# Routing arithmetic placed in fewer attention steps, lane marks spread over more of them, and the first expert gathers issued one step later

## What is computed

```python
def attn(x):                       # one head, no mask
    q, k, v = x @ wq.T, x @ wk.T, x @ wv.T
    q, k = rope(q), rope(k)        # the first token is not rotated
    w = softmax(q @ k.T / sqrt(128))
    return (w @ v) @ wo.T

def ffn(z):
    for _ in range(2):
        zn = rmsnorm(z) * norm_w
        scores = softmax(zn @ router_w)
        top2 values, normalised to sum 1 -> cw (per token and expert)
        z = z + sum_e cw[:, e] * ((silu(zn @ w1[e]) * (zn @ w3[e])) @ w2[e])
    return z

x = x + layernorm(attn(layernorm(x)))
x = x + layernorm(ffn(layernorm(x)))
```

## Time and profile before

| | |
|---|---|
| Time, three runs | 1088.16, 1090.71, 1094.11 us; median 1090.71 |
| Profiled execution | 1088.16 us, span 1086.4 us |
| Busy share of the span | TensorE 91%, VectorE 64%, ScalarE 51%, GpSimd 47% |
| Mean granted TensorE clock | 0.971 |
| Stretch of the change | from about 268 to 378 us, in the span's own time |

### The profile page before, as it was taken

One profiled execution on the slowest core, in us unless ns is written; L12 is line 12 of the kernel. 1 busy time (PEld: TensorE's weight loads), 2 busy tenths in 40 slices (PEclk: granted clock), 3 DMA queues, 4 the chain that ended last, 5 costly groups with the idle time before them and its releaser, 6 DMA issues.

```text
span 1086.4 us, 22670 instructions
## 1 busy us (share of the span) xinstructions
PE 988.0 (91%) x7114; PEld 682.0 (63%) x7114; DVE 696.0 (64%) x1628; ACT 551.9 (51%) x1075; POOL 508.3 (47%) x671
## 2 busy tenths in 40 slices
PE   4899998869999899999999999999989999999930
PEld 2578877547787667666667765667656666666620
DVE  5879987958998555784435567545596333856336
ACT  3566666538888645433334564345644333333313
POOL 2412233775777763434443354443434444554315
PEclk9999999979999999999999999999999999999975
DMA  9900000000000144334336445356344335746342
GB/s 309 368 21 0 0 0 1 1 5 25 16 19 15 31 112 121 90 78 99 88 106 167 132 116 129 88 137 175 76 117 125 89 93 130 204 106 155 81 158 93
DMA packets 137350, 105.28 MB, mean 97 GB/s; under 512 B 84528, under 2 KB 124080, under 8 KB 137264
## 3 DMA queue, kind: packets, MB, share of 16 engines
q1 hardware_dynamic: 123632, 66.88, 23.6%
q0 software_dynamic: 13632, 37.24, 11.6%
HBM read 54.27 MB, written 31.20 MB: 79 GB/s over the span
## 4 chain that ended last, share of the span: by engine, by line
PE 78%; DVE 13%; issue 3%; POOL 2%; ACT 2%; DMA 1%; SPq 0%; DVEq 0%; ACTq 0%; POOLq 0%
PE psum_s L830 32%; PE psum_o L2042 16%; PE psum_s L1557 6%; PE psum_s L2031 5%; PE psum_o L1597 4%; PE psum_t L1552 4%; PE psum_o L1592 3%; PE psum_t L676 2%; PE psum_s L1534 2%; DVE arena L1337 1%; PE psum_t L2006 1%; DVE arena L1849 1%; PE psum_y L1584 1%; DVE arena L1317 1%; DVE arena L1332 1%
## 5 line engine op out<-in xcount | busy, mean ns | idle before, releaser
L830 PE MATMUL psum_s<-w_all,arena 128*128 x1704 | 391.9, 380 | 1.6 <-issue 0.8
L1737 POOL DMA_INDIRECT token_rows<-arena,result_row_of_row x142 | 144.9, 1020 | 313.1 <-ACT arena L1814 310.1
L830 PEld LDWEIGHTS psum_s<-w_all,arena 128*128 128x128 f16 x1704 | 158.1, 98 | 180.4 <-issue 5.0
L2042 PE MATMUL psum_o<-w_all,arena 128*128 x1704 | 209.3, 273 | 10.4 <-DVE arena L1971 10.4
L815 DVE SCALAR_TENSOR_TENSOR arena<-psum_s,gate_scale,arena 128x512 f32<-128x512 f32 x142 | 106.5, 750 | 155.9 <-PE psum_s L830 154.4
L2042 PEld LDWEIGHTS psum_o<-w_all,arena 128*128 128x128 f16 x1704 | 164.7, 98 | 54.3 <-issue 15.5
L1971 DVE TENSOR_TENSOR arena<-psum_s,arena 128x512 f16<-128x512 f32 x142 | 97.8, 689 | 130.9 <-ACT arena L1807 130.5
L1814 ACT ACTIVATE arena<-psum_o 128x256 f32<-128x256 f32 x142 | 54.4, 383 | 233.7 <-PE psum_o L2042 233.7
L791 POOL DMA_INDIRECT arena<-sorted_rows,token_of_row x142 | 141.3, 995 | 55.8 <-issue 41.5
L809 ACT ACTIVATE arena<-psum_s,silu_scale 128x512 f32<-128x512 f32 x142 | 97.6, 687 | 101.7 <-PE psum_s L830 101.7
L1807 ACT ACTIVATE arena<-psum_s 128x512 f16<-128x512 f32 x142 | 84.7, 597 | 28.0 <-PE psum_s L2031 21.8
(11 more groups left out here) (276 smaller groups left out, 1234.9 us busy)
## 6 DMA issues: line engine op xcount, KB each, us to landing
w_all<-in_L_ffn_w SPq DMA_DIRECT2D x24, 512.0 KB, 10.0
arena<-token_rows SPq DMA_DIRECT2D x48, 256.0 KB, 3.5
sorted_rows<-w_all SPq DMA_DIRECT2D x24, 256.0 KB, 2.3
out<-x_sb SPq DMA_DIRECT2D x8, 512.0 KB, 3.0
arena<-token_rows SPq DMA_DIRECT2D x8, 512.0 KB, 7.5
arena<-sorted_rows,token_of_row POOLq DMA_INDIRECT x142, 3.2
arena<-arena SPq DMA_TRANSPOSE x142
token_rows<-arena,result_row_of_row POOLq DMA_INDIRECT x142, 2.4
```

The lines of the kernel that those rows point to most:

```text
L830: last = nc.tensor.matmul(bank, e_xT[:, u, lx * DC + c, :], w_split[:, bass.ds(e * EW + at, FF)], start=(q == 0), stop=(q == 3 * DC - 1))
L1737: nc.gpsimd.indirect_dma_start(rows, bass.IndirectOffsetOnAxis(ap=targets[:, at : at + 1], axis=0), y_row[:, u, :], None).then_inc(s_sent[ ...
L2042: last = nc.tensor.matmul(psum_e, hT[:, lh, c, :], w_split[:, bass.ds(e * EW + at, D)], start=(q == 0), stop=(q == 3 * FC - 1))
```

## The change

VectorE's routing work gets other places in its own instruction order, with the same instructions:

| Behind step | before | after |
|---|---|---|
| 3 | `tiles_before`, split | `tiles_before`, `expert_starts`, `expert_rows_of_tiles`, split |
| 4 | `expert_starts`, split | `rows_of_tokens`, `experts_of_tiles`, `mark_tiles`, split |
| 5 | `expert_rows_of_tiles`, split | split, 4 lane marks |
| 6 | `rows_of_tokens`, `experts_of_tiles`, split | split, 4 lane marks |
| 7 | `mark_tiles`, 2 lane marks, split | split, 4 lane marks |
| 8 to 12 | split, 6 lane marks each | split, 4 lane marks each |

The steps of a hardware loop (`dve.Fori`) are 8 to 12 before and 5 to 12 after. On GpSimd, the three first gathers stand behind `normalise(NT + 13, ...)` instead of `normalise(NT + 12, ...)`.

```diff
@@ GpSimd
                 normalise(NT + i, FIRST_SPLITS + 2 * (i + 3) if i < NT - 2 else None)
                 for j in FIRST_ROWS[i + 3]:
                     first_rows(j)
-                if i == NT - 4:
+                if i == NT - 3:
                     for n in range(UNROLL):
                         fetch(pool, n)
@@ VectorE
             step(NT + 3, True, True, True, True, False, 0, read_counts)
             tiles_before(dve, link, 0)
+            expert_starts(dve, link, 0)
+            expert_rows_of_tiles(dve, link, 0)
             split_lo(odd(3))
             step(NT + 4, True, True, True, True, False, 1)
-            expert_starts(dve, link, 0)
-            split_lo(odd(4))
-            step(NT + 5, True, True, True, True, False, 2)
-            expert_rows_of_tiles(dve, link, 0)
-            split_lo(odd(5))
-            step(NT + 6, True, True, True, True, False, 3)
             rows_of_tokens(dve, link, 0)
             experts_of_tiles(dve, link, 0)
-            split_lo(odd(6))
-            step(NT + 7, True, True, True, True, False, 4)
             dve.wait_ge(s_rows, 1)
             dve.wait_ge(s_marks, 7)
             mark_tiles(first_hot_t, TILES)
-            mark_lanes(first_hot_p, 0, 2)
-            split_lo(odd(7))
-            with dve.Fori(8, 13) as i:
+            split_lo(odd(4))
+            with dve.Fori(5, 13) as i:
                 step(NT + i, True, True, True, True, False, i - 3)
                 split_lo(odd(i))
-                mark_lanes(first_hot_p, 6 * i - 46, 6)
+                mark_lanes(first_hot_p, 4 * i - 20, 4)
             step(NT + 13, True, True, True, True, False, 10)
```

## The result

The changed kernel took 1104.33 us at the median of 6 runs (1101.51 to 1106.18); the kernel before, on the same chip in turn, took 1091.02 (6 runs, 1086.72 to 1094.11). The ratio is 1.0124, 95% interval 1.0096 to 1.0152: slower by 13.3 us between the medians, where 9.7 were forecast. The time of 1104.33 lies inside the range of 1094 to 1105, near its upper end, but above the 1097.5 to 1102 that the terms of the sum allow. The profiled execution took 1106.44 us (span 1104.7).

A forecast was written before the change was run, and what follows sets the result against it. TensorE, 78% of the chain that ended last, was taken to bound the kernel. Bunching 4.9, late gathers 3.2 and clock 1.6 summed to +9.7 us, on the median of 1090.71 giving 1100 us, range 1094 to 1105.

The forecast's parts named there:

- The bound, and the credit of VectorE: Second attention pass: TensorE bounds at 7.84 us a step; VectorE, 7.5 us a step, has almost no credit for lateness.
- The rival that TensorE's slack absorbs the bunch: Steps 4 and 5 don't stretch despite VectorE's lateness; +3.8 us, 1094.5; chance 0.08, 0.03 more with gathers hidden too.
- Step 4 (3.9 late): Fifth-numbered attention step, `step(NT + 4)`: blocks moved ahead of it make TensorE's projection L1584 start 3.9 us late.
- part one: The bunching of VectorE's routing work in the second attention pass: +4.9 us, bounds 4.2 and 5.6.
- Step 5 (another 1.9): Attention step `step(NT + 5)`: VectorE's blocks behind the previous step delay TensorE's projection L1584 by another 1.9 us.
- A fall of the clock in step 4 would be free: Attention step `step(NT + 4)`: a lower TensorE clock costs nothing, since the next step waits for VectorE anyhow.
- Gathers late (+3.2): Hand-over to the experts: gathers start 7.9 us later, tile 0 arrives late, first expert's transposes +3.2 us, bounds 2.6 and 3.8.
- TensorE could have started at 372.6: Hand-over: with tile 0 ready, TensorE starts the first expert tile at 372.6, being 373.52 less the 0.92 us wait.
- the rival with hidden gathers: Hand-over: tile 0 arrives before 372.6 and the 0.92 us wait is saved; +4.0 us, 1095; chance 0.11.
- The clock (+1.6): First expert tile: after over 5 us without matmul, TensorE's clock is lower for 3.3 us; +1.6 us, bounds 0 and 2.
- Lateness feeds itself: Rival: clock falls in steps 4 and 5 too, VectorE's loop starts late; some 3 us more, 1103.5; chance 0.08.
- everything shifts alike: After the first expert tile: experts are bound by TensorE, so the delay carries through unchanged.

The follow-up runs named there:

- vector_only: Against the kernel before: only VectorE's new order, the first gathers left in their old place; 1101.87 us against 1095.34, ratio 1.0060.
- vector_only_port_free: Against vector_only: one GpSimd weight split (L918, L922) issued behind `first_rows`, away from the moved VectorE blocks; one run, 1101.92 us.
- starts_only: Against the kernel before: only `expert_starts` moved, from behind step 4 to behind step 3; one run, 1100.52 us.
- gathers_in_gap: Against the kernel before: the three first gathers moved into GpSimd's wait for ScalarE inside `normalise(NT + 13)`; one run, 1092.98 us.
- spread_one_by_one: Against spread_and_gap: the three first gathers also spread, one in each of two `normalise` gaps, one behind a weight split; 1094.96 us, ratio 0.9992 to the kernel before.
- before_again: The kernel before, unchanged, traced a second time to see the scatter; one run, 1091.60 us.
- gathers_only: Against the kernel before: only the three first gathers moved one step later, VectorE's order kept; 1100.12 us against 1095.34, ratio 1.0039.
- gathers_only_filler: Against gathers_only: 48 unused identity matmuls added on TensorE ahead of the first expert tile; 37.76 us from step 14 to the first expert's transposes.
- spread_and_gap: Against the kernel before: VectorE's routing blocks spread behind steps 4 to 8, first gathers in GpSimd's gap inside `normalise`; 1091.45 us, ratio 0.9997.

## Why the prediction was right, and what was off

- **The bound, and the credit of VectorE: right.** What VectorE does late in step 4 reaches TensorE in full. The rival that TensorE's slack absorbs the bunch is out: vector_only alone costs 6.7 us. One slip: 3.9 + 1.9 - 1.0 is 4.8, not 4.9.
- **Step 4 (3.9 late): mechanism right, mis-sized.** It was 5.9. The step that failed is the sentence that "such small dependent instructions run back to back" at the durations of the earlier trace rows. Those rows are from moments at which GpSimd had only one-column instructions or none; moved to 268.90, the block runs beside L943, L918 and L922 of GpSimd and waits for each. vector_only_port_free shows it, and leaves 4.75 us for the rest of part one. The Trainium skill has this rule (SBUF — State Buffer, Who interferes with whom): a VectorE instruction with two SBUF inputs, or one in a two-port mode, which a copy can enter, and a GpSimd instruction that reads SBUF lock each other out: the one that is issued first holds the other up for its whole length. The trace agrees, with ends 0.03, 0.02 and 0.14 us apart. Not having asked what GpSimd does at the new place is the omission of the prediction.
- **Step 5 (another 1.9): right.** From L1577 in step 4 to that in step 5 it is 289.06 - 279.27 = 9.79 us, and I had 286.9 - 277.2 = 9.7. The sign that I had named, a wait of nearly 2 us at L1577, isn't there: TensorE, slowed by the lower clock, arrived together with VectorE, whose L1349 ended at 288.58 + 0.28 = 288.86. At full clock it would have been there at 279.27 + 7.84 = 287.11 and waited.
- **Steps 6 to 13 without waits, four marks for six worth nothing: right.** From L1577 of step 5 to step 14 it is 66.27 us; before, 348.36 - 281.89 = 66.47.
- **A fall of the clock in step 4 would be free: right here,** and only because VectorE sets step 5; starts_only, where it doesn't, paid 1.4 us for it.
- **Gathers late (+3.2): right.** Counted as before (6.97 less, since step 14 starts at 355.33 and not 348.36) they start at 370.42, predicted 370.5. The transposition comes 3.30 behind (3.44), its data are used 3.45 behind that (2.9, bounds 2.3 and 3.44). The first L830 so stands at 377.17, not 376.9. ScalarE's L1069 has no wait for GpSimd ahead of it any more, as forecast:

```profile
373.59 0.58 ACT L1069 ACTIVATE arena<-psum_y,arena 128x256 f32<-128x256 f32 x1
```

- **"TensorE could have started at 372.6": nearly right, without effect on the sum.** In the kernel before, removing the 0.92 us of L1584 alone would have won nothing, since the last weight split held the start (gathers_in_gap). In the changed kernel the split comes ahead of the gathers; attention ends at 378.60, which is 371.63 by the times of before, and with the 0.38 us of spread_one_by_one TensorE could have started at 372.0. So the rival with hidden gathers fell by the length of the chain, 3.30 + 3.45 us behind 370.42, as the prediction argued.
- **The clock (+1.6): right mechanism, too small.** The first tile took 390.54 - 384.14 = 6.40 us instead of 3.94: 2.5. I had taken the 3.3 us at the lower level of the earlier trace rows, after a stretch with 1.10 us of work in four; after 5.55 us without any, the lower level lasted for about 5 us. The bound of 2 was too tight.
- **The sum.** 4.8 + 2.0 for the waits behind GpSimd, 3.2 + 0.3 - 0.2 (the tile in 3.94 and not 4.1) for the gathers, 2.5 for the clock: 12.6 us, the 12.61 of the traces.
- **The range: held by its margin.** 12.6 us is more than the +11.4 to which the terms could add up; that 1104.33 lies inside 1094 to 1105 it owes to the 3 us added for scatter. The nearest number on record is that of the rival *Lateness feeds itself*, 1103.5, and this is luck: its clock did fall in step 4, but that cost nothing, and its loop with a slow first pass cost nothing either (66.27 us behind step 5). The excess came from GpSimd's instructions, 2.0, and from the clock in the hand-over, 0.9.
- **After the first tile "everything shifts alike": not quite, and open.** The profiled executions drift apart by 5.6 us more, mostly in four jumps of 1.5, 1.4, 0.6 and 1.6 us at about the 6th, 24th, 75th and 95th tile. Ahead of the first of them ScalarE was idle for 3.72 us, and the profile names nothing of this core as its releaser:

```profile
413.05 0.60 ACT L1800 ACTIVATE arena<-psum_s 128x512 f16<-128x512 f32 x1 [3.72 <-remote]
```

before_again was also to tell whether these jumps are scatter, and it has none, which by its expectation would lay them on the edit. The other traces don't bear this out. gathers_only has jumps of 1.3 and 0.9 us at the 24th and 95th tile, while gathers_only_filler, with the same edit, has none there, nor has spread_and_gap; spread_one_by_one, which up to there is no slower than the kernel before, has both. The medians need only 0.7 us of all this (13.3 against 12.6), and vector_only, whose trace has 1.3 and 1.5 there, is 6.6 us slower by its ratio, not more than the 7.0 of its two stretches. So it seems to be a matter of the single execution rather than of the edit; what causes the jumps stays open.

## What to carry to other kernels

When a block of small VectorE instructions is moved, its durations don't move with it: lay the queue of GpSimd beside the new place, and add for each tensor instruction there up to its whole length. This was seen on instructions whose operands all lie in SBUF; those that read PSUM, L1337 and L1349, took 1.21 to 1.22 and 0.28 to 0.29 us in every row read here, beside L943 and L918 too. Price a wait of TensorE by two numbers, the wait and the slower work after it, and ask for the second whether another engine already sets what follows. Before crediting a removed wait, look for the next thing that the same instruction needs, here the last weight split of the kernel before, which held the same start back when the wait that the profile named was gone.

## What was unexpected of the hardware

- An 8-element copy of VectorE took 0.59 us and an 8-element operation 0.89 beside a 128x256 and a 128x512 operation of GpSimd, instead of 0.17; a 128x128 one 1.12 instead of 0.29. GpSimd's own instruction lost at most 0.12 us there (L922 1.28 against 1.16). Where VectorE's was first, it was the other way round: in the kernel before, L922 at 370.78, issued just behind VectorE's L1293 (370.66, 0.73 us), took 1.63 us.
- 5.55 us without a matmul brought the granted clock to 0.50 before the work resumed, and it stayed there for about 5 us of work: the tile's first six products took 2.74 us against 1.47. Filling the place with 5.5 us of unneeded matmuls kept it at 1.00.
- A transposing DMA inside SBUF, issued by SyncE, is used 3.45 us after its issue. In the kernel before, the traffic behind it paused 2.3 us after the issue; the windows of the changed kernel show no such pause, so how the 3.45 us divide isn't shown.
